# Inverting 64x64 triangular blocks: the diagonal 16x16 blocks on VectorE instead of three levels on TensorE

## What is computed

```python
M = where(stril, einsum('bhncd,bhnmd->bhncm', k_beta, k) * decay, 0)
T = solve_triangular(eye + M, eye, lower=True)       # 64x64 per chunk and head
v_c = einsum('bhnij,bhnjd->bhnid', T, v_beta)
k_cumdecay = einsum('bhnij,bhnjd->bhnid', T, k_beta * exp(g)[..., None])
def step(state, inp):                                # 8 chunks, one after the other
    attn = einsum('bhcd,bhed->bhce', q_i, k_i) * dec_i
    v_new = v_i - einsum('bhcd,bhde->bhce', kcd_i, state)
    out_i = einsum(..., q_i * exp(g_i), state) + einsum('bhce,bhed->bhcd', attn, v_new)
    state = state * exp(g_last) + einsum(..., k_i * exp(g_last - g_i), v_new)
    return state, out_i
```

## Time and profile before

| | us |
|---|---|
| median of 3 runs (2472.37 to 2474.38) | 2473.27 |
| profiled execution, from the first to the last instruction | 2469.4 |
| one round in the middle (1204.0 to 1274.0) | 70.0 |
| PE / POOL / DVE / ACT busy over the span | 97% / 70% / 66% / 59% |
| share of PE in the chain that ended last | 85% |

### The profile page before, as it was taken

One profiled execution on the slowest core, in us unless ns is written; L12 is line 12 of the kernel. 1 busy time (PEld: TensorE's weight loads), 2 busy tenths in 40 slices (PEclk: granted clock), 3 DMA queues, 4 the chain that ended last, 5 costly groups with the idle time before them and its releaser, 6 DMA issues.

```text
span 2469.4 us, 101468 instructions
## 1 busy us (share of the span) xinstructions
PE 2389.2 (97%) x44496; PEld 1851.1 (75%) x44496; DVE 1630.4 (66%) x2859; ACT 1458.0 (59%) x3270; POOL 1729.3 (70%) x1774
## 2 busy tenths in 40 slices
PE   3899999999999999999999999999999999999898
PEld 2687777777877777778777777788777777787554
DVE  5666676667666676677666766776667666765422
ACT  3766666666666656666666566666666666665211
POOL 2777777778777777788777777887777777887200
PEclk9999999999999999999999999999999999999999
DMA  3211111111111101111111011111111011111100
GB/s 101 54 37 35 44 23 30 35 44 31 37 39 35 44 11 43 35 44 31 33 44 35 25 28 44 31 39 37 35 44 29 24 35 44 31 38 27 51 18 17
DMA packets 71048, 90.13 MB, mean 36 GB/s; under 512 B 16720, under 2 KB 39376, under 8 KB 70480
## 3 DMA queue, kind: packets, MB, share of 16 engines
q1 hardware_dynamic: 70608, 83.63, 13.0%
HBM read 78.53 MB, written 5.08 MB: 34 GB/s over the span
## 4 chain that ended last, share of the span: by engine, by line
PE 85%; ACT 7%; DVE 3%; issue 2%; POOL 1%; DMA 1%; SPq 0%; POOLq 0%; DVEq 0%; ACTq 0%
PE ps_two L438 10%; PE ps_state L413 10%; PE ps_two L413 9%; PE ps_p L651 6%; PE ps_p L473 5%; PE ps_p L468 5%; PE ps_p L591 4%; PE ps_state L615 3%; PE ps_p L564 3%; PE ps_p L599 3%; PE ps_state L651 2%; PE ps_p L487 2%; PE ps_state L487 2%; PE ps_two L640 2%; PE ps_p L700 2%
## 5 line engine op out<-in xcount | busy, mean ns | idle before, releaser
L1206 POOL TENSOR_TENSOR Sd<-St,el 128x512 f32<-128x512 f32 x192 | 201.2, 1048 | 441.7 <-DVEq L1105 441.6
L1245 POOL TENSOR_SCALAR on<-idx_s,lutb 128x134 f32<-128x134 int32 x480 | 355.6, 744 | 27.1
L1084 DVE TENSOR_SCALAR Vn<-ps_p,bR 128x128 f32<-128x128 f32 x512 | 167.8, 350 | 209.2 <-PE ps_p L564 134.9
L968 DVE SCALAR_TENSOR_TENSOR cacc<-ps_two,cw,cacc 128x1022 f32<-128x1022 f32 (+2 forms) x192 | 245.6, 1279 | 44.5 <-ACT cacc L738 39.4
L968 DVE SCALAR_TENSOR_TENSOR cacc<-ps_state,cw,cacc 128x1022 f32<-128x1022 f32 (+2 forms) x192 | 245.7, 1279 | 39.5 <-ACT cacc L738 34.8
L413 PE MATMUL ps_state<-xnT,w_qkv 128*128 128x256 f32 x1024 | 256.1, 393 | 5.9 <-DVEq L973 5.9
L438 PE MATMUL ps_two<-xnT,w_z 128*128 128x512 f32 x512 | 259.0, 618 | 0.3 <-DVE sqk L1047 0.3
L413 PE MATMUL ps_two<-xnT,w_qkv 128*128 128x256 f32 x1024 | 251.3, 389 | 0.0
L1051 DVE STREAM_TRANSPOSE XW<-XW 128x1024 f32<-128x1024 f32 x160 | 199.3, 1246 | 36.5 <-DVE XW L1061 31.5
L853 ACT ACTIVATE Xs<-XW 64x512 f32<-64x512 f32 x320 | 201.2, 629 | 17.9 <-DVE XW L1061 10.2
L413 PEld LDWEIGHTS ps_state<-xnT,w_qkv 128*128 128x128 f32 x1024 | 185.2, 190 | 32.5 <-DVEq L973 6.3
(11 more groups left out here) (171 smaller groups left out, 6040.7 us busy)
## 6 DMA issues: line engine op xcount, KB each, us to landing
qg<-g_scratch SPq DMA_DIRECT2D x64, 512.0 KB, 7.2
g_st<-g_scratch SPq DMA_DIRECT2D x64, 256.0 KB, 5.9
w_qkv<-in_wqkvz SPq DMA_DIRECT2D x16, 512.0 KB, 3.7
w_z<-in_wqkvz SPq DMA_DIRECT2D x16, 256.0 KB, 3.1
w_o<-in_wout SPq DMA_DIRECT2D x16, 256.0 KB, 2.6
idx_s<-in_idx SPq DMA_DIRECT2D x32, 67.0 KB, 1.8
fw_scratch<-looked_up SPq DMA_DIRECT2D x32, 67.0 KB, 1.7
Kg<-in_x SPq DMA_DIRECT2D x2, 1024.0 KB, 5.6
```

Source lines behind the costliest of these rows:

```text
L968: dve.scalar_tensor_tensor(dst, both[n][:, :, 0:S - t], cw[:, kind, 3 - t:4 - t], dst, ALU.mult, ALU.add).then_inc(s["taps"], 1)
L1206: pool.tensor_tensor(Sd[:, :, :, :], St[:, c % 2, :, :, :], el[:, R.par, :, :, c].unsqueeze(3).broadcast_to([P, BB, RATIO, P]), ALU.mult). ...
L1245: m = pool.tensor_scalar(slots[k], idx_s[:, :], float(k), lutb[:, k:k + 1], ALU.is_equal, ALU.mult)
```

## The change

Levels 1 to 3 of the doubling leave PE. In their place DVE inverts all diagonal blocks of 16x16 of a round (128 of them, one per partition) in a chain of instructions called `small_blocks`. It gathers the diagonal blocks of U, moves them by 32x32 transposes so that each partition holds one block of 16x16 in `G`, and inverts there: four tiny products and sums for blocks of 4, then for 8 and for 16 two rounds each of products (`product`, all terms into `terms`) and sums over rows (`total`). Transposes bring the result back, and four `tensor_scalar` write W and then X. PE keeps the levels 4 and 5.

The order of a round follows. Four projections instead of one stand ahead of the first product. The last `turn_back` of a round moves from the next `begin` to behind these projections, in bank 4, and DVE's last `gated` moves behind `small_blocks` and a first tap. Output blocks, projections and z get other places and banks. `clear_inverse` goes.

```diff
-LEVELS = 6
+LEVELS = (4, 5)
...
-PROJ_AT = {(1, 1): 1, (2, 0): 2, (2, 1): 3, (3, 0): 4, (3, 1): 5, (4, 0): 6, (4, 1): 7}
-OUT_AT = {(1, 0): 0, (1, 1): 1, (2, 1): 2, (3, 1): 3}
-Z_AT = {(4, 1): (0,), (5, 0): (1,), (5, 1): (2,)}
+PROJ_FIRST = (0, 1, 2, 3)
+PROJ_AT = {(4, 1): (4, 5), (5, 0): (6, 7)}
+OUT_AT = {(4, 0): (1,), (4, 1): (2,), (5, 1): (3,)}
+Z_AT = {(5, 1): (0, 1, 2)}
...
-    outs = [] if first else spread([("out", i) for i in range(4)], (6, 4, 5, 4))
+    outs = [] if first else [(("ot3", 0), 4)] + spread([("out", i) for i in range(4)], (5, 4, 5, 4))
...
             def invert(R):

                 if R.nxt:
-                    proj(R, 0)
-                for lv in range(1, LEVELS):
-                    pe.wait_ge(s["xs"], R.at(2 * lv, 0, 11))
+                    for i in PROJ_FIRST:
+                        proj(R, i)
+                if R.before() is not None:
+                    turn_back(R.before(), 3)
+                    outputs(R, "out", R.before(), 0)
+                for n, lv in enumerate(LEVELS):
+                    pe.wait_ge(s["xs"], R.at(1 + 3 * n, 0, 5))
...
+            def small_blocks(R):
...
+                dve.scalar_tensor_tensor(blocks[:, :, :], u[:, :, 2 * BASE:], in_half[1], u[:, :, 0:2 * BASE], ALU.mult, ALU.add
...
+                dve.transpose(by_block[:, :, :], turned_blocks).then_inc(base, 1)
...
+                dve.scalar_tensor_tensor(g, by_block[:, :, 0:BASE], in_block[0], by_block[:, :, BASE:], ALU.mult, ALU.add
...
+                dve.memset(G[:, 0:BASE * BASE:BASE + 1], 1.0).then_inc(base, 1)
...
+                dve.tensor_tensor(t4, g4[:, :, 2 * BASE:2 * BASE + 2], g4[:, :, 3 * BASE + 2:3 * BASE + 3].broadcast_to([P, 4, 2]),
+                                  ALU.mult).then_inc(base, 1)
+                dve.wait_ge(base, R.at(5, 0, 20))
+                dve.tensor_tensor(c3, c3, t4, ALU.add).then_inc(base, 1)
...
+                def product(out, left, right, n):
+
+                    return dve.tensor_tensor(out.rearrange("p (i k j) -> p i k j", k=n, j=n),
+                                             left.rearrange("p j k -> p k j").unsqueeze(1).broadcast_to([P, n, n, n]),
+                                             right.unsqueeze(2).broadcast_to([P, n, n, n]), ALU.mult)
+
+                def total(out, n, size):
+
+                    return dve.tensor_reduce(out, terms[:, 0:size].rearrange("p (x j) -> p x j", j=n), mybir.AxisListType.X, ALU.add)
...
+                product(terms[:, :], g[:, 8:16, 0:8], g[:, 8:16, 8:16], 8).then_inc(base, 1)
+                dve.wait_ge(base, R.at(15, 0, 20))
+                total(Y[:, :], 8, 512).then_inc(base, 1)
...
+                for q in range(2):
+                    m = dve.tensor_scalar(by_block[:, :, q * BASE:(q + 1) * BASE], g, in_block[q], None, ALU.mult)
+                m.then_inc(base, 1)
+                dve.wait_ge(base, R.at(19, 0, 20))
+                dve.transpose(turned_blocks, by_block[:, :, :]).then_inc(base, 1)
...
+                for q in range(2):
+                    m = dve.tensor_scalar(x[:, :, q, :], blocks[:, :, :], in_half[q], None, ALU.mult)
+                m.then_inc(xs, 1)
+
+            turned_blocks = blocks[:, :, :].rearrange("p s (h i) -> p i (s h)", h=2)
...
             def invert(R):
...
+                of = R.before()
+                if R.nxt:
+                    taps(R, 0, (1,))
+                if of is not None:
+                    gated(of, 3)
+                if R.nxt:
+                    taps(R, 0, (2, 3))
+                if of is not None:
+                    outputs(R, "out", of, 0)
+                second_products(R, 4, 3)
+                turn()
```

More of the change, by code:

```diff
@@ L86, in constants @@
 def constants():
-    j, i = np.arange(P)[:, None] % C, np.arange(C)[None, :]
-    cols = [np.eye(P), np.ones((P, P)), (j == i) * 1.0]
-    for lv in range(LEVELS):
+    row = np.arange(P)[:, None]
+    j, i = row % C, np.arange(C)[None, :]
+    cols = [np.eye(P), np.ones((P, P))]
+    for lv in LEVELS:
         n = 1 << lv
@@ L94, in constants @@
     cols.append(np.where(i >= j, 0.0, NEG))
+    cols += [(row // 32 % 2 == q) * 1.0 for q in range(2)] + [(row % 2 == q) * 1.0 for q in range(2)]
     cols.append(np.broadcast_to(np.array([LN_EPS, RMS_EPS, -0.5, 0.5]), (P, 4)))
@@ L160, in build @@
         P1 = sb("P1", [P, BB, NC, C])
+        blocks = sb("blocks", [P, SLOTS, 2 * BASE])
+        by_block = sb("by_block", [P, BASE, 2 * BASE])
+        G = sb("G", [P, BASE * (BASE + 1)])
+        terms = sb("terms", [P, SLOTS * 2 * BASE])
+        Y = sb("Y", [P, 64])
         Kg = sb("Kg", [P, BB, NC, P])
@@ L478, in products, with begin @@
                 right.then_inc(banks[1][1], 1)
-            def begin(R, last=None):
+            def begin(R):
                 pe.wait_ge(s["silu"], R.at(0, 4, 4))
@@ L494, in begin @@
                     m.then_inc(filled, 1)
-                if last is not None:
-                    turn_back(last, 3)
                 for i in range(4):
@@ L675, in body @@
                 if R.nxt:
-                    begin(R.following(), last=R)
+                    begin(R.following())
                 else:
@@ L838, in invert @@
-                if not R.nxt:
-                    gate(R, 0)
-                    gate(R, 1)
+                if R.nxt:
+                    tap0(R, 0)
+                values(R, 1)
+                if R.nxt:
+                    tap0(R, 1)
+                swap(R, 0)
+                first_products(R, 4)
+                if R.nxt:
+                    silu(R, 0)
+                swap(R, 1)
+                if R.nxt:
+                    tap0(R, 2)
+                else:
+                    gated_unit(0, 0, AHEAD[0])
@@ new lines, in invert, with first_products @@
+                first_products(R, 5)
+                if R.nxt:
+                    silu(R, 1)
+                    tap0(R, 3)
+                    silu(R, 2)
+                    gate(R, 0)
+                    silu(R, 3)
+                else:
+                    gated_unit(1, 1, AHEAD[1])
+                    gated_unit(2, 2, AHEAD[2])
+                    gate(R, 0)
+                gate(R, 1)
+            def first_products(R, lv):
+                done = [wait_full(act, R, "p1", (lv, b))[1] for b in range(BB)]
+                n = 1 << lv
+                even = P1[:, :, :, :].rearrange("p b c (q d n) -> p b (c q) d n", d=2, n=n)[:, :, :, 0, :]
+                act.activation(even, ps_p1[:, :, 0:S // 2].rearrange("p b (q n) -> p b q n", n=n), ACT.Copy
+                               ).then_inc(done[0], 1)
+                wait_read(act, R, "p1", (lv, 0))
+                act.sem_inc(done[1], 1)
@@ L868, in body @@
                     i = c // 2
-                    if c == NC - 1 and R.nxt:
-                        for b in range(BB):
-                            wait_full(act, R, "vn", (NC - 1) * BB + b)
-                        clear_inverse()
                     bank, _ = wait_full(act, R, "o", i)
@@ L1123, in gated @@
                     wait_read(dve, R, "z", 3)
-                bank, done = wait_full(dve, R, "ot", i)
+                bank, done = wait_full(dve, *place_of_turn(R, i))
                 dst, src = (t[:, i].rearrange("p b a t -> p (b a t)") for t in (hT, z))
```

185 lines of the change are left out of this document (108 added, 77 removed).

## The result

| | before | after |
|---|---|---|
| median of the four timed runs, us | 2472.82 (2470.60 to 2474.38) | 2663.03 (2662.30 to 2670.76) |
| profiled execution, first to last instruction, us | 2469.4 | 2660.5 |
| mean granted clock of TensorE | 0.995 | 0.918 |
| a steady round, us | 70.0 | 75.03 |

The changed kernel takes 1.078 times as long, with an interval of 1.0763 to 1.0793: 190 us more, 5.9 per round. The forecast was 2670.

A forecast was written before the change was run, and what follows sets the result against it. PE was taken as the bound. Per round, -6.4 us of products, +11.7 of waiting and +0.9 of clock give +6.2, times 32 +198 us: 2670 us, with its own range 2590 to 2825 and an 8-in-10 range 2355 to 2800.

The forecast's parts named there:

- What is removed: Six of a round's ten product blocks leave PE, 1.07 us each: 6.4 us less per round.
- S = D - 9.6: PE's loss per round, S, is the time from the DVE chain's start until W is written, D, less 9.6 us.
- The second wait: PE waits some 2 us for the turned output's bank, which DVE frees by gating after X and one tap.
- Break-even at D = 16: The change gains only while DVE's chain has W written in under 16.0 us (9.6 + 6.4).
- D without disturbance: DVE's chain until W is written, with no waiting for POOL: 12.2 us, bounds 10.3 to 14.
- D with POOL beside it: DVE's two-tensor instructions take turns with POOL's by whole instructions: chain 12.6 + 8.7 = 21.3 us, 19.7 to 24.4.
- (a): Rival: DVE's chain takes no turns with POOL, D = 12.2, 2350 us (2290 to 2410); chance 0.20.
- (b): Rival: only DVE instructions of 256 columns and more take turns, D = 15.2, 2448 us; chance 0.08.
- (c): Rival: DVE's one-tensor tensor_scalars also wait out POOL's look-ups, D = 24.8, 2783 us; chance 0.14.
- The clock: After PE's long wait, 5 us at half rate each round, costing 0.9 us (bounds 0 and 2.5).
- The sum: Per round -6.4 + 11.7 + 0.9 = +6.2 us, times 32 +198 us, forecast 2670 us.
- Other things moved: POOL's look-ups and turns, SyncE's load of w_o and the gate values z: counted at nothing.

The follow-up runs named there:

- e4: The changed kernel with POOL's look-ups ahead of its key and attention products and DVE's gating ahead of the first tap: 2343.8 us.
- e1: The changed kernel without POOL's four key and two attention products of a round, that computation left out: 2400.0 us.
- e2: The changed kernel with POOL's look-ups ahead of its key and attention products, into a buffer of their own: 2403.1 us.
- e6: The changed kernel with POOL's key products held until DVE has finished the chain's last product of 512 columns: 2587.0 us.
- e10: The changed kernel with DVE's gating ahead of the first tap, plus 11 overwritten matmuls in PE's wait for W: 2605.6 us.
- e5: The changed kernel with each of POOL's four key products of a round split into two halves: 2634.6 us.
- e8: The changed kernel with 9 more matmuls per round, overwritten later, in PE's wait for W: 2671.4 us.
- e3: The changed kernel with DVE's gating that frees the turned output's bank moved ahead of the first tap: 2636.3 us.

## Why the prediction was right

**What is removed.** 6.4 us per round were counted for six product blocks. PE's busy time fell by more: from 69.85 to 62.60 at the full clock in e4, and to 62.08 in the change, if the lost 2.36 are taken off its 64.44. The term was 0.9 to 1.4 too small, and not by the price of a block: counted from the start of one matmul to the start of the next, the products fell by 6.2, from 9.9 to 3.7 (before against e4). The rest lies in work that was counted as unchanged and stands beside fewer products now: projections 14.9 to 14.1, z 7.75 to 7.4.

**The formula S = D - 9.6.** With D of 12.2 (e1), 12.5 (e2) and 20.7 (the change) it gives 2.6, 2.9 and 11.1. The two waits sum to 2.75, 3.0 and 10.4, and in the last the first product itself is 0.9 longer, 1.93 instead of 1.07, at the lower clock, which fills part of the second wait: 11.3 in all. So it held. The second wait, 2 in the prediction, was 0.89 mostly for that reason. Break-even at D = 16 has e1 and e2 on its faster side, e6 (17.3) and the change on its slower one. But the clock is left out of it: e2 gains 2.1 us per round and e6 loses 3.6, and a straight line between them crosses zero at some 14.3 (an estimate; no run lies there). And that what follows is hidden holds only where PE comes there late, by the second wait or the clock: with the gating first and at the full clock, in e4 and e10, PE waits 0.9 and 0.2 us more for DVE's taps.

**D without disturbance.** 12.2 was taken, 12.17 measured in e1, but the parts were not as told. The gather beside the q scaling has a turn in it (1.35 in most rounds instead of 0.68; it ends 0.55 after POOL's scaling). Sums over rows of eight cost nothing beyond their columns (0.69 for 512, where I left 0 to 1.3 more open), two transposes cost 1.04 to 1.08 where 1.31 was counted, and the products of 512 took 1.01 to 1.04 where 0.69 was, with up to 0.6 more left open. That the sum agrees to 0.03 is luck: the errors cancel, within the bounds given.

**D with POOL beside it.** 12.6 us until the eighth turn ends, then 8.7. Measured in the round shown: the pair of 64 ends at 1235.70, 12.8 after the start, and 7.9 more to W. The tiny products stand at 1.2 to 1.82 where 1.3 to 1.9 were foretold. e1 and e2 confirm that the waiting is for POOL's two-tensor products, e5 that it goes in turns by whole instructions. But one sentence of that step is wrong: that DVE instructions with one tensor in SBUF show none of this. The row that I leaned on, L908 beside L1173, had a POOL instruction of one tensor. I put the harmlessness down to DVE's side where it belonged to POOL's. e6 shows the same tensor_scalars waiting until two-tensor products are over.

**Rivals.** (a), no turns, is out: it would have been right for the order of e2, which measured 2403 instead of its 2350. (b), only the large ones wait, is out: 8 columns wait as 256 do. (c), tensor_scalars wait out look-ups, is out as told (0.43 in the mean for 256 columns beside look-ups); beside key products, in e6, these instructions do wait. The Trainium skill, page "SBUF — State Buffer", section "Who interferes with whom", counts `tensor_scalar` among the operations that can contend for the pair of ports shared with GpSimd, and says that `tensor_reduce`, the sum over rows, never does on this chip; e6 agrees on the first (1.67 in the mean), e5 on the second (0.29). The same section of the Trainium skill has a DVE instruction with two inputs in SBUF contend with a GpSimd instruction that reads SBUF; with the look-ups, which read one tensor from there, e2 shows next to none of it (0.17 to 0.32 for 8 columns, 0.15 to 0.17 in e1).

**The clock.** 0.9 per round was taken, between 0 and 2.5. The lower clock reached 5.6 us past the wait, where 5 were foreseen. PE's rows lose more, 2.4 in steady rounds and 3.2 in the mean. Of the 2.4, 0.9 lies on the first product, within S, which leaves 1.5; e10 puts the part on the path at about 1.0 for the kernel with the gating first, and for the change's steady round it was not isolated, since e8 left other waits. But what a round of the change loses beyond 2.4 is on the path. This one has the same waits, 9.5 and 0.9:

```profile
229.70:307.90 78.20, 67.63 (x995) 53.54 (x994) 59.85 (x99) 37.84 (x92) 54.47 (x56) 0.89 0.13 34
```

Against the steady round it loses 5.7 instead of 2.4 and is 3.2 longer.

**The sum.** -6.4 + 11.7 + 0.9 = +6.2 per round was forecast, +5.9 measured. In the steady round shown it is +5.0: -7.8 of work (69.85 to 62.08), +10.4 of waiting (0.15 to 10.59) and +2.4 of lost clock. So the removal was sized 1.4 too small, and waiting with clock (12.8 against 12.6) nearly right. What cancels the first miss is luck: not all rounds are steady, which I had not foreseen. Eleven of 31 took 76 to 81 us. In the mean of the 30 rounds after the first, 0.7 us more is lost to the clock than in the steady one, by longer low stretches, and 0.4 more is waited, most of it in six waits of 0.8 to 3 us at `keys_through`, line 575 (10.7 us), which the trace puts down to issue. Why these come in some rounds and not in others is open.

**Other things moved.** POOL, ACT and SyncE were counted at nothing, and no wait of PE on them returns round by round. But the place of the gating behind a tap, which I priced correctly as part of S, was a choice of the new order that cost 27 us by itself (e3).

## What to carry to other kernels

Before a chain of many short instructions goes to VectorE, look at what GpSimd runs beside it in those microseconds: beside products of two tensors each link costs a whole GpSimd instruction, beside one-tensor instructions its own length, and reordering GpSimd may decide the sign (here 2663 against 2403 us). When two explanations of an undisturbed row differ by which side of a pair matters, look for a row that has the other side changed before leaning on it. And count lost clock only as far as no other engine's wait stands right behind it: 3.3 us of work lost to it cost some 1 us per round in e3, a loss of 1.7 at most 0.2 in e4, and in e1 each further us lost cost one.
